# Small products of ones ahead of TensorE's waits in the head of a fused attention and mixture-of-experts kernel

## What is computed

```
xn  = layernorm(x)
q, k, v = xn Wq' + bq, xn Wk' + bk, xn Wv' + bv
kv  = cumsum over length of (elu(k) + 1) * v
x   = x + ((elu(q) + 1) * kv) * scale  Wo' + bo
xn2 = layernorm(x)
top 2 of 8 experts by xn2 @ router_w, softmax of the two logits
y   = sum over the two of score * (silu(g) * u) @ w2[e],  g, u = split(xn2 @ w1[e])
y  += (silu(xn2 @ w_gate) * (xn2 @ w_up)) @ w_down          (the shared expert)
out = x + y
```

## Time and profile before

| | us |
|---|---|
| median of three runs | 377.15 |
| profiled execution, whole | 377.39 |
| its span, first to last instruction | 375.7 |
| TensorE busy in it | 340.8 (91%) |
| TensorE's weight loads | 252.9 (67%) |
| VectorE / ScalarE / GpSimd busy | 235.5 / 214.5 / 189.3 |
| mean granted TensorE clock | 0.976 of full |

### The profile page before, as it was taken

One profiled execution on the slowest core, in us unless ns is written; L12 is line 12 of the kernel. 1 busy time (PEld: TensorE's weight loads), 2 busy tenths in 40 slices (PEclk: granted clock), 3 DMA queues, 4 the chain that ended last, 5 costly groups with the idle time before them and its releaser, 6 DMA issues.

```text
span 375.7 us, 9015 instructions
## 1 busy us (share of the span) xinstructions
PE 340.8 (91%) x2868; PEld 252.9 (67%) x2868; DVE 235.5 (63%) x579; ACT 214.5 (57%) x385; POOL 189.3 (50%) x293
## 2 busy tenths in 40 slices
PE   7866599999997999999999899999999999999980
PEld 6655488787786878878888555655566566656660
DVE  5977976687766886798677655464544533443430
ACT  3767639666775686876526345544545545455440
POOL 4823085578586775937134532453353534434432
PEclk9998989999998999999999999999999999999995
DMA  7976052337355462464845826647475676695530
GB/s 194 384 190 201 15 130 64 76 91 227 56 149 191 106 198 67 115 199 142 253 154 164 159 54 100 96 70 109 76 111 85 100 101 87 97 109 88 84 49 0
DMA packets 77467, 46.41 MB, mean 124 GB/s; under 512 B 61040, under 2 KB 72560, under 8 KB 77040
## 3 DMA queue, kind: packets, MB, share of 16 engines
q1 hardware_dynamic: 63088, 35.08, 37.0%
q0 software_dynamic: 9664, 10.71, 17.6%
q10 hardware_dynamic: 4672, 0.07, 0.9%
HBM read 19.09 MB, written 12.97 MB: 85 GB/s over the span
## 4 chain that ended last, share of the span: by engine, by line
PE 46%; POOL 18%; DVE 10%; issue 9%; DMA 7%; ACT 7%; POOLq 1%; SPq 1%; DVEq 0%; ACTq 0%
PE bU L1027 13%; PE bG L1027 12%; PE bV L1048 6%; POOL x_rows L570 6%; PE bQ L1048 6%; DMA xs<-bo 3%; PE bK L1007 2%; DMA xT<-rows 2%; PE bU L237 2%; PE bG L237 2%; DVE ab L1475 1%; DMA stage<-in_w_expert 1%; DVE st L1352 1%; POOL y L510 1%; POOL nt L517 1%
## 5 line engine op out<-in xcount | busy, mean ns | idle before, releaser
L1475 DVE SCALAR_TENSOR_TENSOR ab<-bU,sg 128x512 f32<-128x512 f32 x64 | 44.1, 689 | 77.0 <-PE bU L1027 52.2
L761 POOL DMA_INDIRECT out_y<-xs,dst_row x32 | 50.0, 1562 | 60.2 <-DMA out_y<-xs,dst_row 39.2
L1158 ACT ACTIVATE sg<-bG 128x512 f32<-128x512 f32 x64 | 37.9, 593 | 45.4 <-PE bG L1027 26.6
L1027 PE MATMUL bG<-we,work 128*128 (+1 forms) x216 | 52.6, 380 | 1.7 <-DVE wd L1531 1.7
L1027 PE MATMUL bU<-we,work 128*128 (+1 forms) x216 | 52.6, 379 | 0.0
L1302 ACT ACTIVATE ws_h<-ab 128x512 f16<-128x512 f32 x36 | 22.7, 629 | 41.6 <-DVE ab L1475 40.1
L570 POOL DMA_INDIRECT x_rows<-rows,slot_u x32 | 35.1, 1098 | 21.3 <-DVE slot_u L1526 10.7
L1751 DVE TENSOR_TENSOR ws_h<-ab,ws_h 128x512 f16<-128x512 f32 x36 | 25.0, 694 | 20.7 <-ACT ws_h L1302 20.7
L1165 ACT ACTIVATE ah<-ab 128x512 f16<-128x512 f32 x32 | 20.1, 628 | 26.9 <-DVE ab L1475 26.8
L1027 PEld LDWEIGHTS bG<-we,work 128*128 128x128 f16 (+1 forms) x216 | 20.7, 99 | 21.2 <-issue 3.6
L1027 PEld LDWEIGHTS bU<-we,work 128*128 128x128 f16 (+1 forms) x216 | 19.8, 99 | 17.4
(11 more groups left out here) (321 smaller groups left out, 813.8 us busy)
## 6 DMA issues: line engine op xcount, KB each, us to landing
stage<-in_w_expert SPq DMA_DIRECT2D x24, 512.0 KB, 4.6
we<-in_w_shared SPq DMA_DIRECT2D x3, 1024.0 KB, 10.7
xs<-bo POOLq DMA_DIRECT2D x8, 256.0 KB, 3.9
out_y<-xs SPq DMA_DIRECT2D x8, 256.0 KB, 2.5
xs<-in_x SPq DMA_DIRECT2D x1, 1280.0 KB, 19.7
x_rows<-we SPq DMA_DIRECT2D x9, 134.0 KB, 2.4
xs<-in_x SPq DMA_DIRECT2D x3, 256.0 KB, 4.3
work<-x_rows SPq DMA_TRANSPOSE x40, 3.2
```

Of the source, the lines that this page charges most:

```text
L761: pool.indirect_dma_start(out_rows, bass.IndirectOffsetOnAxis(ap=dst_row[:, b:b + 1], axis=0), ya[b % NY], None, bounds_check=NT * P - 1, ...
L1027: ins = pe.matmul(dst[t * n:(t + 1) * n, :], x2[:, hi * KC + k, t * n:(t + 1) * n], w[t][lo][:, k, half, :], start=s == 0 and k == 0, stop ...
L1158: act.activation(sg[q][:], src[:], ACT.Silu, scale=1.0 / WS).then_inc(S["sg_done"], 1)
L1475: dve.scalar_tensor_tensor(out=ab[q][:], in0=src[:], scalar=1.0 / WS, in1=sg[q][:], op0=ALU.mult, op1=ALU.mult).then_inc(S["a_done"], 1)
```

## The change

`warm` gets a second argument, the bank that it writes (bR unless told otherwise), and its products now go to the last 128 columns of that bank instead of the first 128. It is called at eleven more places of TensorE's list in the head, each right ahead of a wait, with 7 to 22 products, 139 in all. Each product is one weight load and one product of 128 columns, of ones. The banks are such that no one else has open work in them at that point. Before `turn_first(0)` stands one more wait, for GpSimd's `pow1`. Nothing is changed on any other engine.

```diff
-            def warm(n):
+            def warm(n, dst=bR):
                 for _ in range(n):
-                    pe.matmul(bR[:, 0:P], ones16[:], ones16[:], start=True, stop=True)
+                    pe.matmul(dst[:, 3 * P:4 * P], ones16[:], ones16[:], start=True, stop=True)
...
                     if i <= 2 and m == 0:
                         for s, (w, lo) in enumerate(((wh, 0), (wl, 0), (wh, 1))):
                             if s == 2:
+                                if i == 2:
+                                    warm(12, bQ)
                                 pe.wait_ge(S["l1_done"], i + 1)
...
                     if s == 2:
+                        if i == 1:
+                            warm(10)
                         pe.wait_ge(S["cxl_done"], i + 1)
...
                             if s == 2:
+                                if n == 2 and m == 0:
+                                    warm(16, bT)
                                 pe.wait_ge(S["sh_lo"], 3 * (n // 2) + m + 1)
...
             warm(48)
             pe.wait_ge(S["const_pool"], 4)
+            pe.wait_ge(S["pow1"], 1)
+            warm(10)
             turn_first(0)
+            warm(8)
             project(0, "kv")
             turn_first(1)
+            warm(7)
             project(0, "q")
             project(1)
+            warm(16)
             attend_out(0)
             turn_first(2)
+            warm(8, bQ)
             project(2)
+            warm(10)
             attend_out(1)
+            warm(22)
             route(0)
             pe.wait_ge(S["const_pool"], 6)
             gate_up(0, 0)
             gate_up(0, 1)
+            warm(20, bD)
             ranks(0)
```

## The result

| | before | after |
|---|---|---|
| median of 13 runs each, us | 376.57 (375.6 to 379.9) | 374.54 (373.44 to 375.96) |
| profiled execution, whole | 377.39 | 373.95 |
| its span | 375.7 | 372.3 |
| mean granted clock in it | 0.976 | 0.993 |

The ratio of after to before is 0.9929, with a 95% interval of 0.9904 to 0.9955: faster by 2.7 us (1.7 to 3.6). Forecast was 1.24 us. The medians differ by 2.03 us.

A forecast was written before the change was run, and what follows sets the result against it. Bound: a chain of releases that enters TensorE at the router and `gate_up(0, 0)`, otherwise mostly DMAs, GpSimd, ScalarE and VectorE. First fall 1.24 us, all else 0: 377.15 - 1.24 = 375.9 us, range 374.0 to 377.4.

The forecast's parts named there:

- The added products cost 0: In TensorE's waits in the head: at 0.055 us a product every group ends inside its wait, so 0.
- The first fall: Clock at 0.50 from 33.70 to 37.12 us, around `gate_up(0, 0)`: it goes, `nt` starts earlier, 1.24 us gained.
- The whole list moves by 1.24: VectorE's list from `nt` on, with the chain to 61.41 us and beyond, comes 1.24 us early.
- The second fall: Clock at 0.50 from 47.36 to 50.77 us: it goes, hidden behind GpSimd's indirect DMAs, 0; bounds 0 and 1.71 us.
- the third: Clock at 0.50 from 115.62 to 119.04 us, no products added, TensorE not in the chain: 0; bounds -1.71 and 0.
- The sum: Whole kernel: 377.39 - 1.24 - 0 - 0 = 376.15 us against the profiled execution, 375.9 against the median.
- B: Rival: TensorE bounds the kernel, both falls in the head count in full, 374.0 us; chance 0.21.
- The sign given for it: Start of the expert part moved by 3 us, to speak for TensorE as the bound.
- C: Rival: nothing reaches the end; the clock falls anyway or a later transfer or queue takes the gain, 377.15 us; chance 0.13.
- D: Rival: clock at 0.50 on reaching `attend_out(1)`, added groups overrun, router and slots late, 379.3 us; chance 0.06.
- The early groups: Groups of 10, 8, 7, 16, 8 and 12 products up to `project(2)`: inside their waits, cost 0.

The follow-up runs named there:

- e12: Kernel before plus 36 products of 8 columns, 20 ahead of `ranks(0)` and 16 in `gate_up(0, 2)`; 375.8 us, ratio 0.9962.
- e13: The change with 7 products in place of 20 ahead of `ranks(0)`, 126 in all; 376.91 us, ratio 0.9993.
- e3: The change with only its six groups up to `project(2)` and the wait for `pow1` kept; 376.16 us, ratio 0.9972.
- e6: The change without the groups of 10, 10 and 22 products ahead of the router; 375.42 us, ratio 0.9948.
- e7: The change without the 20 products ahead of `ranks(0)` and the 16 in `gate_up(0, 2)`; 374.89 us, ratio 0.9938.
- e2: Kernel before plus only the 20 products ahead of `ranks(0)` and the 16 in `gate_up(0, 2)`; 375.76 us, ratio 0.9956.
- e8: Kernel before with only a comment added, as a control and second profile; 377.24 us, ratio 0.9994.
- e10: The change with all products of ones 512 columns wide and a quarter as many, 49 against 48 in before; 376.81 us, ratio 0.9981.
- e11: The change with only its 61 products up to `project(2)` cut to 8 columns; 375.51 us, ratio 0.9937.
- e4: The change plus 30 products between `gate_up(3, 0)` and `gate_up(3, 1)`; 374.65 us, ratio 0.9937 to before.
- e9: The change with its 139 products cut from 128 to 8 columns, the first 48 left at 128; 375.91 us, ratio 0.9948.
- e1: Kernel before plus only the groups of 10, 10 and 22 products ahead of the router; 377.36 us, ratio 1.0002.
- e5: The change without its six groups up to `project(2)` and without the wait for `pow1`; 377.62 us, ratio 0.9993.

## Why the prediction was wrong in size

*The added products cost 0.* As time on TensorE this held to the hundredth: 22 products took 1.39 us and 20 took 1.28, so 0.055 for each further one, and every group ended inside its wait. But **this is the step that failed**: the prediction began from "products of ones can only act on two things: the clock, and the time that they take themselves". It weighed the 139 products as time on the engine only, put them at 0 and gave no bound below. Their 278 instructions move every later fetch of TensorE's code, and one of these had been lying on the end of the last load of expert weights, the very transfer on which the start of the expert part hung. That term was worth -1.2 us (the 1.18 of wait), not 0. e12 gets it with 72 instructions and no held clock, e13 loses it with 26 fewer. The wait was to be read in the profile of before, as 1.18 us ahead of `wd`, 1.67 us ahead of the first expert product and 5.28 us of `stage<-in_w_expert` in the chain; my reading of the chain stopped at 162 us.

*The first fall: -1.24.* Right as a mechanism and, in one execution, in size: from 26 us to `nt` the change gains 1.26 us, e13 1.24, e3 1.24, e6 and e7 1.25, with `ab` early and the stall behind it for `y`. The profiles of e2 and e12, which have a fall at 33 us as before has, gain 0.2 and 0.1 there. "The whole list moves by 1.24" was less right: at 59 us the change has kept all of it (1.34), but e3, e6, e8, e10, e11 and e13 only 0.80 to 0.93. The rest goes in GpSimd's small steps of the layernorm behind its four indirect DMAs: from the fourth of these to the end of `shift` (L527) it takes 4.2 to 4.3 us before, after and in e7, and 4.6 to 4.7 in those six, where one step more takes 0.6 to 0.7 us instead of 0.2; why is open. And e8 gains 1.24 there as well, with nothing changed, because the falls lie elsewhere in every execution. The kernel before already has this gain in a part of its runs, so it could not count for 1.24 on the median. Streaming alone (e10) gave 0.7 us (-0.3 to 1.7), the size of what was left of this term together with anything the early falls cost.

*The second fall: 0, the third: 0.* Nothing measured speaks against either, to about 1 us. e7 has the second fall in its profile and the change's span to 0.3 us; e4's runs have hardly a fall and gain nothing on the change.

*The sum.* -1.24 was forecast. The profiled pair differs by 3.44: 0.49 ahead of the change's first effect (e8 has 0.39 of it, with no edit, so it belongs to the execution), 1.26 the first fall, 0.34 between `nt` and 184.5 (0.08 of it by 59 us), 1.37 the code. The runs differ by 2.7: by e9 and e10 2.0 of code and 0.7 of streaming. The 2.0 is more than the 1.2 that the wait for `wd` accounts for; e9's profile has 0.57 us more at 184.5, where the wait described below is missing, and whether the code does that isn't shown.

*The rivals.* B, TensorE as the bound, had the time almost right (374.0) and the reason wrong: by it the second and third fall would count. The sign given for it, a start of the expert part 3 us early, did come (3.46), and would have misled: the 1.37 us of it that no fall of the clock explains is the code's. C was too pessimistic. D, the late products, did not occur in any profile: at 1.00 all groups were in time.

*The early groups* I took for harmless. Their profiles (after, e3, e4, e6, e7, e13) have no fall between 8 and 15 us, and e1, e2, e5 and e12 have one:

```profile
8.00:14.80 6.80, 6.11 (x42) 4.75 (x41) 5.93 (x19) 4.25 (x8) 4.84 (x11) 0.75 0.99 353
```

That is e5's; the change's is this:

```profile
8.00:14.80 6.80, 6.22 (x61) 5.01 (x59) 6.49 (x20) 4.77 (x9) 4.92 (x11) 1.00 0.97 363
```

In e2 and e5 VectorE is 0.5 to 0.6 us later than in after at 22 us, in e1, with two stretches, 2.1. But e8, e9, e11 and before itself show no early fall without these groups' streaming, and e4, which has the streaming and no fall, is 1.2 us later than after at 22 us, so something else moves that point too. How much of the 0.7 us belongs here and how much to the first fall stays open.

*What else stays open.* That the place of a fetch makes or ends the wait is shown by e12 and e13, which moved it both ways. What is held are some of the load's 16 counts (nine in before) and not its data; why a piece there holds them is not shown, and no profile has a piece between 0.8 and 3.1 us behind the issue. The 1.05 us that e8 loses between 150 and 184.5 against before, at a clock of 1.00, is the wait of the router's products for the transposed rows of the last batch: 1.75 us in e8, 0.70 before, 0.33 after, 0 in e6, e7, e9 and e12. The place of the nearest piece does not tell these apart (0.7 us behind the issue of the transposes in e9 and in e11, whose wait is 1.10), so this cause is open.

## What to carry to other kernels

Instructions that cost an engine nothing still have a place in its code: when padding, unrolling or a trace marker changes the count, look at which waits for a DMA appear or vanish far from the edit, and change the count alone (products of 8 columns) as a control before you give the gain to the mechanism intended. Take a second profile of the same program before a feature of the first, such as where the clock falls, is priced as if every run had it. And read the chain to its end, above all at the borders between parts, where a single late transfer holds up all.

## What the runs showed of the hardware

- TensorE's instructions come in by pieces of 16 KB, 25 or 26 in this kernel, each 0.9 to 2.4 us on its queue, half of them at most 1.1. One that meets another transfer can delay its user by 0.9 to 1.2 us (weights) or about 2 us (the two transposes, 5.6 to 5.9 us from issue to use in place of 3.9).
- A load's data and the report of it are two things: with a piece of code at its end, the last of its 16 semaphore counts stood 1.7 to 2.0 us behind its last packet of data (4 profiles), otherwise 0.5 to 0.9 (11 profiles).
- The Trainium skill ("Runtime: NRT & Kernel Launch", Instruction fetch mechanics) has blocks of 16 KiB and calls their cost mostly hidden. The trace agrees on the size (16384 bytes each) and, before, on the cost for the engine itself: no wait of TensorE over 0.15 us lies at one of the 25 pieces. For the transfers beside it the cost isn't hidden.
- The clock's stretches at 0.50 are 3.4 us long, or twice that, and lie at different places in each execution of one program: 33.7, 47.4 and 115.6 us in one of before, 40.5 alone in another. The mean clock of single runs of the kernel before went from 0.963 to 0.993.
